# Attention and feed-forward block on one core: the inverse softmax sums spread by DMA instead of by selector matmuls

## The reference, cut to what matters

```python
xn = layernorm(x)
h = (xn - mean) * rsqrt(var + eps) * ln_scale + ln_bias
c_q, c_kv = h @ w_down_q.T, h @ w_down_kv.T              # 64 latents each
q, k, v = heads(c_q @ w_up_q.T), heads(c_kv @ w_up_k.T), heads(c_kv @ w_up_v.T)   # 16 heads of 64
q, k = rope(q), rope(k)
attn = softmax(q @ k.T / 8)
att = concat(attn @ v) @ w_out.T + xn
y = square(relu(xn @ W_fc.T)) @ W_proj.T
mem = 0; five times: mem = 0.9 * mem + y - (mem > 1); spikes += mem > 1
out = x + att + spikes / 5
```

## Time and profile before

| | |
|---|---|
| median of 3 runs | 1083.81 us (1083.73 to 1083.85) |
| the profiled execution's own time | 1083.63 us |
| its span, first to last instruction | 1081.8 us |
| busy: TensorE / VectorE / ScalarE / GpSimd | 1041.4 / 898.9 / 930.0 / 895.9 us |
| DMA | 217.96 MB, 201 GB/s over the span |
| mean granted TensorE clock | 0.993 of full speed |

### The profile page before, as it was taken

The page is one execution under the profiler, slowest core; times in us unless marked ns, Lnnn a source line. Parts: engine busy times, 40 slices in busy tenths (PEclk is TensorE's granted clock), DMA queues, the critical chain, the costliest instruction groups (busy, mean ns, idle before and its releaser), DMA issues.

```text
span 1081.8 us, 26191 instructions
## 1 busy us (share of the span) xinstructions
PE 1041.4 (96%) x6880; PEld 700.7 (65%) x6880; DVE 898.9 (83%) x1223; ACT 930.0 (86%) x3136; POOL 895.9 (83%) x897
## 2 busy tenths in 40 slices
PE   3789999999999999999999999999999999999987
PEld 2556666666666666666666666666666666666654
DVE  3798888898888889888889888889888888888872
ACT  3789988988998888999898999898899889898861
POOL 3777989888888888888898888988888988888851
PEclk9899999999999999999999999999999999999999
DMA  5388777877877877777887777787777787777773
GB/s 178 106 227 207 204 209 202 223 211 200 205 208 204 230 203 207 206 202 202 219 215 207 203 203 209 201 228 208 199 208 206 203 229 204 210 195 196 207 193 81
DMA packets 93281, 217.96 MB, mean 201 GB/s; under 512 B 22464, under 2 KB 43200, under 8 KB 93120
## 3 DMA queue, kind: packets, MB, share of 16 engines
q1 hardware_dynamic: 92864, 216.52, 75.5%
q10 hardware_dynamic: 384, 1.05, 0.4%
HBM read 7.77 MB, written 4.19 MB: 11 GB/s over the span
## 4 chain that ended last, share of the span: by engine, by line
PE 80%; issue 6%; DVE 6%; SPq 3%; ACT 2%; DMA 2%; ACTq 0%; DVEq 0%; POOL 0%; POOLq 0%
PE ps_s L328 20%; PE ps_u L342 20%; PE ps_b L447 10%; PE ps_qk L318 8%; PE ps_a L383 5%; PE ps_a L396 5%; PE ps_qk L319 4%; SPq L254 3%; PE ps_b L413 2%; DVE turned L703 2%; DVE qk L687 2%; PE ps_a L355 1%; PE ps_a L360 1%; PE ps_b L456 1%; PE ps_a L367 1%
## 5 line engine op out<-in xcount | busy, mean ns | idle before, releaser
L538 ACT ACTIVATE prob<-ps_s,neg_max 128x256 f32<-128x256 f32 x1024 | 475.0, 486 | 41.0 <-DVE neg_max L692 38.2
L837 POOL TENSOR_TENSOR partner<-partner,rope_sb 128x512 f32<-128x512 f32 x256 | 327.1, 1278 | 108.3 <-DMA partner<-raw 108.3
L692 DVE TENSOR_REDUCE neg_max<-ps_s 128x4 f32<-128x1024 f32 x256 | 310.8, 1214 | 116.9 <-PE ps_s L328 115.4
L840 POOL TENSOR_TENSOR qk<-qk,partner 128x512 f32<-128x512 f32 x256 | 326.5, 1275 | 20.1
L703 DVE STREAM_TRANSPOSE turned<-prob 128x1024 f32<-128x1024 f32 x256 | 316.4, 1236 | 2.3 <-ACT prob L538 1.3
L328 PE MATMUL ps_s<-qk 64*128 64x256 f32 x2048 | 292.4, 404 | 3.5 <-ACT prob L538 2.4
L342 PE MATMUL ps_u<-gathered,ckv 128*64 128x256 f32 x2048 | 278.4, 393 | 3.1 <-DMA gathered<-turned 2.8
L328 PEld LDWEIGHTS ps_s<-qk 64*128 64x128 f32 x2048 | 177.5, 187 | 106.0 <-issue 86.5
L538 ACT ACTIVATION_READ_ACCUMULATOR prob<-ps_s,neg_max 128x1 f32 x1024 | 221.8, 217 | 0.0
L550 ACT COPY raw<-ps_qk 128x512 f32<-128x512 f32 x256 | 154.1, 602 | 67.0 <-PE ps_qk L319 66.9
L342 PEld LDWEIGHTS ps_u<-gathered,ckv 128*64 128x64 f32 x2048 | 124.8, 136 | 107.8 <-issue 52.6
(11 more groups left out here) (67 smaller groups left out, 897.5 us busy)
## 6 DMA issues: line engine op xcount, KB each, us to landing
gathered<-turned SPq DMA_DIRECT2D x1016, 128.0 KB, 2.4
partner<-raw SPq DMA_DIRECT2D x256, 256.0 KB, 2.4
x_sb<-in_x SPq DMA_DIRECT2D x32, 128.0 KB, 2.3
resid<-early SPq DMA_DIRECT2D x32, 128.0 KB, 2.0
out<-out_sb SPq DMA_DIRECT2D x32, 128.0 KB, 2.1
turned<-in_wup SPq DMA_DIRECT2D x2, 512.0 KB, 5.7
gathered<-turned ACTq DMA_DIRECT2D x8, 128.0 KB, 4.0
rope_sb<-in_rope SPq DMA_DIRECT2D x1, 512.0 KB, 6.8
```

Of the source, the lines that this page charges most:

```text
L538: last = nc.scalar.activation(prob[:, s % 2, :, h, :, t, :].rearrange("p j k c -> p k j c"), ps_s[:, s % 2, h, t, :].rearrange("p (k j c) ...
L692: nc.vector.tensor_reduce(neg_max[:, s % 2, :, :], ps_s[:, s % 2, :, :, :], AXIS_X, ALU.max, negate=True).then_inc(max_ready, 1)
L837: nc.gpsimd.tensor_tensor(other, other, sin_sb, ALU.mult).then_inc(sin_ready, 1)
L840: nc.gpsimd.tensor_tensor(qk[:, s % 4, :, :], qk[:, s % 4, :, :], other, ALU.add).then_inc(rope_done, 1)
```

## The change

The sums go another way. VectorE takes the reciprocal in step 0 of the block and transposes its 32 columns; SyncE writes the 128 rows of 32 numbers to a tensor in memory outside (`keep_rows`, step 1) and reads them back with two DMAs, each giving the same 8 KB to 64 partitions (`spread_rows`, step 3). All eight pairs' inverse sums then stand in `spread`. GpSimd multiplies in steps 7, 0, 1 and 2; TensorE's output products come in step 1 (one chunk), step 4 (two) and step 6 (one). The selector matmuls, the transposes, their copies on ScalarE and the split on GpSimd go, and with them the load of the selectors. The core of the diff:

```diff
-        den = sb("den", [P, 2, TT, H])
-        rden = sb("rden", [P, TT, H])
-        rden_hl = sb("rden_hl", [P, TT, P], F32R)
-        rden_t = sb("rden_t", [P, S], F32R)
-        sel_sb = sb("sel_sb", [P, PAIRS, P], F32R)
+        den = sb("den", [P, 2, H, TT])
+        rden = sb("rden", [P, TT * H])
+        rden_t = sb("rden_t", [P, 32])
-        spread = sb("spread", [P, 2, 2, S])
+        spread = sb("spread", [P, PAIRS, S])
+        rows_out = nc.dram_tensor("rows_out", (2, H, S), F32, kind="Internal").ap()
...
+            def keep_rows(b, par, i):
+                sp.wait_ge(rows_ready, done(b))
+                if not outside(b - 2, B):
+                    sp.sem_inc(sp_waited, 1)
+                    sp.wait_ge(spread_in[par], 32 * i)
+                sp.dma_start(rows_out[par].rearrange("h (t q c) -> q (h t) c", t=TT, c=32),
+                             rden_t[:, :]).then_inc(rows_kept[par], 16)
+
+            def spread_rows(b, par, i):
+                sp.wait_ge(rows_kept[par], 16 * (i + 1))
+                sp.sem_inc(sp_waited, 1)
+                sp.wait_ge(u_norm, done(CHUNKS * (b - 1) + CHUNKS - 1))
+                for h in range(2):
+                    sp.dma_start(spread[h * L:(h + 1) * L, :, :].rearrange("p j s -> p (j s)"),
+                                 rows_out[par, h * PAIRS:(h + 1) * PAIRS, :].rearrange("j s -> (j s)").unsqueeze(0)
+                                 .to_broadcast([L, PAIRS * S])).then_inc(spread_in[par], 16)
...
+                if not outside(b, B):
+                    if p == 1:
+                        keep_rows(b, b0, i)
+                    elif p == 3:
+                        spread_rows(b, b0, i)
...
             def attention_out(b, c, par):
                 if c == 0:
-                    pe.wait_ge(bc_evac, done(CHUNKS * b + CHUNKS - 1))
+                    pe.wait_ge(final_done, done(b - 1))
...
-                if not outside(b - 1, LAST) and p >= 4:
-                    attention_out(b - 1, p - 4, 1 - b0)
                 if is_last(b):
-                    if p == 2:
-                        transpose_last_rden(b)
-                    elif p == 5:
-                        broadcast_last_rden(b)
-                    elif p == 6:
-                        last_attention_out(b, 0, b0)
-                        last_attention_out(b, 1, b0)
-                    elif p == 7:
-                        last_attention_out(b, 2, b0)
+                    if p == 7:
+                        for c in range(3):
+                            last_attention_out(b, c, b0)
...
-                if p < 4 and not outside(b - 1, LAST):
-                    broadcast_rden(b - 1, p)
                 if not outside(b, B) and p in (2, 3):
                     ffn_out(b, p - 2)
+                if not outside(b - 1, LAST) and p in (1, 4, 6):
+                    for c in {1: (0,), 4: (1, 2), 6: (3,)}[p]:
+                        attention_out(b - 1, c, 1 - b0)
...
-                if p == 7 and not outside(b, LAST):
-                    transpose_rden(b)
...
-            def invert_sums(b, b0):
+            def invert_sums(b, b0, i):
                 dve.wait_ge(exp_done, done(PAIRS * b + PAIRS - 1))
-                dve.wait_ge(rden_split, done(b - 1))
-                nc.vector.reciprocal(rden[:, :, :], den[:, b0, :, :]).then_inc(rden_ready, 1)
+                nc.vector.reciprocal(rden[:, :], den[:, b0, :, :].rearrange("p h t -> p (h t)")).then_inc(rden_ready, 1)
+                dve.wait_ge(rden_ready, done(b))
+                if not outside(b - 1, B):
+                    dve.sem_inc(dve_waited, 1)
+                    dve.wait_ge(rows_kept[1 - b0], 16 * (i + b0))
+                    dve.sem_inc(dve_waited, 1)
+                nc.vector.transpose(rden_t[:, :], rden[:, :]).then_inc(rows_ready, 1)
...
+                if p == 0 and not outside(b, B):
+                    invert_sums(b, b0, i)
                 if is_last(b):
-                    if p == 0:
-                        invert_sums(b, b0)
-                    elif p == 5:
-                        normalise_last(b, 0, b0)
-                        normalise_last(b, 1, b0)
-                    elif p == 6:
-                        normalise_last(b, 2, b0)
+                    if p == 6:
+                        for c in range(2):
+                            normalise_last(b, c, b0, i)
+                    elif p == 7:
+                        normalise_last(b, 2, b0, i)
...
-                if p in (1, 2, 4, 5) and not outside(b - 1, LAST):
-                    normalise_u(b - 1, {1: 0, 2: 1, 4: 2, 5: 3}[p], 1 - b0)
+                if p < 3 and not outside(b - 1, LAST):
+                    normalise_u(b - 1, p + 1, 1 - b0, i - 1 + b0)
+                if p == 7 and not outside(b, LAST):
+                    normalise_u(b, 0, b0, i)
```

More of the change, by code:

```diff
@@ L74, in spike_levels, with build @@
     return levels
-def build(nc, x, wup, wdown, wkv_t, wv, wo_t, ln_cols, wfc_t, wproj_t, rope, ident, sel, out):
+def build(nc, x, wup, wdown, wkv_t, wv, wo_t, ln_cols, wfc_t, wproj_t, rope, ident, out):
     ctx = ExitStack()
@@ L165, in build @@
         s_ready, max_ready, exp_done = sem("s_ready"), sem("max_ready"), sem("exp_done")
-        rden_ready, rden_hi, rden_split = sem("rden_ready"), sem("rden_hi"), sem("rden_split")
-        rt_ready, rt_evac = sem("rt_ready"), sem("rt_evac")
-        bc_ready, bc_evac, u_norm = sem("bc_ready"), sem("bc_evac"), sem("u_norm")
+        rden_ready, rows_ready = sem("rden_ready"), sem("rows_ready")
+        rows_kept = [sem(f"rows_kept{i}") for i in range(2)]
+        spread_in = [sem(f"spread_in{i}") for i in range(2)]
+        u_norm = sem("u_norm")
         out_part = sem("out_part")
@@ L399, in ffn_out @@
                     last.then_inc(y_ready, 1)
[L401 to L431, removed]
             def last_attention_out(b, c, par):
@@ L491, in extras @@
                         latents_by_token(b + 1, 1 - b0)
-                if p < 4 and not outside(b - 1, LAST):
-                    broadcast_rden(b - 1, p)
                 if not outside(b, B) and p in (2, 3):
                     ffn_out(b, p - 2)
+                if not outside(b - 1, LAST) and p in (1, 4, 6):
+                    for c in {1: (0,), 4: (1, 2), 6: (3,)}[p]:
+                        attention_out(b - 1, c, 1 - b0)
                 if not outside(b + 1, B) and p in (5, 6):
                     ffn_in(b + 1, p - 5, 1 - b0)
-                if p == 7:
-                    if not outside(b + 3, B):
-                        transpose_inputs(b + 3, 1 - b0)
+                if p == 7 and not outside(b + 3, B):
+                    transpose_inputs(b + 3, 1 - b0)
                 if p == 7 and isinstance(b, int) and b == -2:
@@ L541, in exponentials @@
                             bias=neg_max[:, s % 2, h, t:t + 1],
-                            accum_out=den[:, bpar, t, 2 * pair + h:2 * pair + h + 1])
+                            accum_out=den[:, bpar, h * PAIRS + pair, t:t + 1])
                 last.then_inc(exp_done, 1)
@@ L557, in copy_u @@
                 nc.scalar.copy(u_sb[:, (s // PAIRS) % 2, pair, :], ps_u[:, 0:S]).then_inc(u_evac, 1)
[L559 to L562, removed]
             def square(n, half):
@@ L604, in relu @@
                                      ps_a[:, :].rearrange("p (c s) -> p c s", c=2), ACT.Relu).then_inc(relu_done, 1)
[L606 to L615, removed]
-                nc.scalar.copy(rden_t[:, :], ps_qk[:, 0, :]).then_inc(rt_evac, 1)
             def move_last(rows):
@@ L628, in copy_value_by_output @@
                 act.wait_ge(setup_pe, 1)
-                nc.scalar.copy(sel_sb[:, :, :], sel_raw).then_inc(setup_act, 1)
                 nc.scalar.copy(wvo_sb[:, 0:PAIRS // 2, :], ps_u[:, :].rearrange("p (j d) -> p j d", d=D))
@@ L643, in step @@
                 b = i * UNROLL + b0
-                if p == 0 and not outside(b - 1, LAST):
-                    copy_rden(b - 1)
-                if is_last(b) and p == 4:
-                    copy_last_rden(b)
                 if not outside(g + LEAD["project"], STEPS):
                     copy_projected(g + LEAD["project"], s + LEAD["project"], i)
-                if p in (1, 2, 3) and not outside(b - 1, LAST):
-                    copy_spread(b - 1, p)
                 if p == 0 and isinstance(b, int) and b == -1:
@@ L657, in step @@
                     copy_u(g, s, i)
-                if p == 0 and not outside(b - 1, LAST):
-                    copy_spread(b - 1, 0)
                 if p == 0:
@@ L744, in integrate, with normalise_last @@
                 ins.then_inc(lif, 1)
-            def normalise_last(b, c, par):
-                dve.wait_ge(bc_ready, done(CHUNKS * b + c))
+            def normalise_last(b, c, par, i):
+                dve.wait_ge(spread_in[par], 32 * (i + 1))
+                dve.sem_inc(dve_waited, 1)
                 dve.wait_ge(u_evac, done(PAIRS * b + 2 * c + 1))
                 two = u_sb[:, par, 2 * c:2 * c + 2, :]
```

(15 more changed lines are left out.)

37 lines of the change are left out of this document (11 added, 26 removed).

## The result

The changed kernel takes 1149.03 us (median of 4, 1145.7 to 1153.2) against 1083.77: a ratio of 1.0605, 95% interval 1.0564 to 1.0646. It is slower, as forecast, but by 65 us instead of 4, outside the range of 1033 to 1112.

What follows compares the result with a forecast made beforehand. TensorE was taken to bound the kernel at 32.08 us per block; afterwards a loop of gathers behind the spread, 32.3. 1083.6 + 7.5 (30 blocks at +0.25) - 3.5 (ends) = 1087.6, stated as 1088 us; range 1033 to 1112.

Steps and rivals of the forecast that it cites:

- TensorE's removed work: Two transposes and four pairs of selector matmuls per block go, 1.60 us, so TensorE would need 30.48 us per block.
- The loop: Once per block, from step 0's weighing of latents through SyncE's queue to the last gather's landing before the next: 32.3 us.
- the median of the gathers: Sign of a right forecast: the gathers' median time from issue to landing rises from 2.4 to over 3.5 us.
- the spread is cheap: Rival, chance 0.22: the spread's megabyte takes 2.3 us or less, TensorE sets 30.48 us per block, time 1032.
- From there the DMA engines decide: Stretch from step 3's exchange to the last gather's landing: 17.4 us of DMA work against 15.2 of issue, landing at 19.2.
- spread 4.5: DMA engines' time for the spread's 1.05 MB per block, at 232 GB/s: 4.5 us.
- the twin: The two wup loads at the trace's start, also 64 partitions of 8 KB each, at 232 GB/s; taken as the spread's rate.
- The same sum without the spread's bytes: The per-block sum over SyncE's queue and the gathers, leaving out the spread's bytes: 30.1 us, below TensorE's 30.48.
- The bound of +0.9: Upper end of the change per block, forecast +0.25 us, between -0.1 and +0.9 with issue and rates at their ends.
- The third rival: Chance 0.15: common 8 KB source and freshly written rows make the spread 5.6 us, block 33.4, time 1120; GpSimd can add.
- I take -3.5 us (between 0 and -6): Term for the last block, where eight selector matmuls, a copy and their waits go: -3.5 us.
- the spread isn't in a hurry there: Claim for the last block: the spread isn't urgent, but shares the DMA engines with the last gathers; no separate size.

Runs made afterwards that it cites:

- e9_thin_act: Changed kernel with each spread DMA cut to 512 bytes per partition and all three added DMAs issued by ScalarE's queue; 1042.51 us.
- e12_half_act4: Changed kernel with 16-bit inverse sums and all three added DMAs issued by ScalarE, the write in step 1 and the spreads in step 4; 1051.20 us.
- e1_thin: Changed kernel with each spread DMA moving 512 bytes instead of 8 KB to 64 partitions, same DMAs, waits and issues; 1060.28 us.
- e16_own64: Kernel before, plus a megabyte loaded in step 3 by two DMAs, 8 KB to each of 64 partitions, each reading its own data; 1124.22 us.
- e2_load3: Kernel before, plus two DMAs in step 3 giving the same 8 KB of an input to 64 partitions each, into an unread tile; 1121.63 us.
- e4_at7: Changed kernel with GpSimd's and TensorE's products in the old steps and the spread issued in step 7 (last block: step 3); 1108.04 us.
- e8_load128: Kernel before, plus a megabyte loaded in step 3 by two DMAs, each giving the same 4 KB to all 128 partitions; 1122.91 us.

## Why the prediction was wrong

**Right by its steps.** The forecast for TensorE's removed work was 1.60 us per block of 32.08. e9_thin_act and e12_half_act4, where TensorE binds, have 30.7 to 30.8, so it is 1.3 to 1.4 (the term was 0.2 to 0.3 too large). The loop is in the trace as written, link by link; the mean is over 20 blocks of the middle:

| link | forecast | block shown | mean |
|---|---|---|---|
| weighing to the end of step 1's projection | 2.8 | 2.82 | 2.82 |
| to the exchange of step 1 | 0.75 | 0.65 | 0.65 |
| to the exchange of step 3, with `keep_rows` | 9.57 | 9.74 | 9.85 |
| to the issue of the last gather (15.2 - 0.63) | 14.57 | 14.71 | 14.83 |
| to its landing (2.4 + 2.2) | 4.6 | 5.62 | 5.18 |
| to the next weighing | 0 | 0.21 | 0.13 |
| sum | 32.3 | 33.75 | 33.45 |

TensorE idles at the place named, the weighing in step 0, for 1.32 and 1.47 us in the rows above. One sign failed: the median of the gathers is 2.8 us, not over 3.5, since only half of them stand behind a spread. The rival "the spread is cheap" fell: 219 GB/s.

**Wrong in the fourth link of the forecast.** "From there the DMA engines decide", 19.2 us, was 20.54 in the block shown (the last three links of the table). The step that failed is the term "spread 4.5", the rate of the twin alone. The bytes move in some 4.8 us, but the landings lie further apart: the exchange in front lands at 521.80 and the second spread at 527.58, 5.8 us later, and the median of 29 blocks is 5.5. That makes the last gather of the block late; the other transfers give back 0.3 us of it. Times from issue to landing of the exchange's second DMA (issued at 519.32), the second spread (520.64) and the last gather (533.47):

```profile
partner<-raw SPq DMA_DIRECT2D x1, 256.0 KB, 2.5
spread<-rows_out SPq DMA_DIRECT2D x1, 512.0 KB, 6.9
gathered<-turned SPq DMA_DIRECT2D x1, 128.0 KB, 5.6
```

The issues were short too: `keep_rows` lengthens the third link from 9.03 us in the kernel before to 9.85, so by 0.8 where I took 0.5. The same sum without the spread's bytes said 30.1 us, and e1_thin, with a sixteenth of them, has 31.3. Together the loop grew by 1.34 us where I had 0.25. The margin is the point: 32.3 lay 0.2 above TensorE's 32.08, so 1.1 us, 3% of the loop, is over four times the forecast's difference. The bound of +0.9 didn't reach it either.

The third rival, "worse than the twin", came out in its size and its period: 5.6 us and 33.4, against 5.5 and 33.4. That was luck as to its reasons. It gave two, that 64 partitions read the same 8 KB and that the rows are freshly written. With own rows (e16_own64) the spread takes 5.5 us too, and so it does with an input that nobody writes (e2_load3). GpSimd's lateness, which it also named, is there, as that of the exchanges behind the spread (1.18 us in the block shown).

**Wrong at the ends.** The span grew by 63.1 us. Thirty periods at +1.34 are 40 of them, where the forecast had 7.5; the other 23 are the ends, for which the forecast had "I take -3.5 us (between 0 and -6)". The periods aren't alike, though. By the transposes of the sums, the 22 periods of the middle hold 29.5 us; the first transpose is 4.3 us later, the first four periods are 13.5 us longer, and the last four with what follows them 15.8. At the end the last block's gathers stand in SyncE's queue behind the late ones, and in the DMA engines behind a spread:

```profile
1112.03 1.98 PE L362 MATMUL ps_u<-gathered,ckv 128*64 128x256 f32 x8 [5.92 <-DMA gathered<-turned]
```

I had written that "the spread isn't in a hurry there" and forgot that what queued behind it in the block before is. A second price comes with the long waits: the granted clock falls. At 162.27 us TensorE has waited 4.42 us for a rotation. Windows of the changed kernel (the third number from the end is the granted clock):

```profile
160.00:170.00 10.00, 7.73 (x44) 5.50 (x46) 4.96 (x7) 4.46 (x16) 9.73 (x9) 0.83 0.69 168
266.00:1000.00 734.00, 675.19 (x4482) 446.81 (x4480) 614.51 (x857) 598.85 (x2044) 606.78 (x572) 1.00 0.92 232
1039.00:1144.90 105.90, 87.01 (x482) 53.21 (x481) 59.56 (x80) 50.29 (x176) 52.61 (x43) 0.85 0.72 174
```

0.83 and 0.85 are means of stretches at 2.4 and at 1.2 GHz. In the middle the clock is full, so the loop's +1.34 us owes it nothing; in the last 105.9 us it is 0.85, against 0.97 in the last 81.8 us of the kernel before. The waits were in the forecast, this price was not. Thin spreads took the three long periods at the end from 35.4, 34.9 and 32.9 us to 31.2, 30.3 and 24.7, so the end hangs on the bytes; what share the clock has in the 23 us was not measured by itself.

## What to carry to other kernels

When work moves from a full engine to DMA, add up the bytes that the same queue carries behind it up to the first transfer that somebody waits for, and close the sum to a loop; an engine's average of free time says nothing. If such a sum lands within a few per cent of the present bound, its error is larger than the difference, and the first and last blocks count as much as the middle. Take for each transfer the time from landing to landing, not its bytes over its rate. Fewer bytes and another issuing engine (16-bit sums, ScalarE's queue, another step) turned this change from +65 to -34 us; moving the same bytes about gave at best +23 (e4_at7).

## What was not expected of the hardware

DMAs to 64 neighbouring partitions moved 219 to 247 GB/s with a common or with separate sources, those to 128 partitions 332 to 413. With 128 partitions reading the same 4 KB (e8_load128) periods from 32.03 to 35.6 us came in turn, where separate sources gave 32.04 to 32.12 in most blocks; why a common source costs there and not with 64 partitions stays open. The chain that ended last put 47% on GpSimd in a kernel in which undoing GpSimd's order of work changed the time by 0.3%, not clearly more than nothing, and moved the chain to SyncE's queue (56%).
